# A latent attention stage with its values in runs of two units, banks split 3+3+2, and query rows laid out by transfers

## What is computed

```python
Wdkv = x @ latent_w + latent_b
q = jnp.einsum('btc,hcl->bhtl', x, Wd_w) + Wd_b[None, :, None, :]
scores = jnp.einsum('bhtl,bsl->bhts', q, Wdkv) / jnp.asarray(np.sqrt(d_head), dtype=x.dtype)
scores = jnp.where(causal[None, None, :, :], scores, -jnp.inf)
attn = jax.nn.softmax(scores, axis=-1)
y = jnp.einsum('bhts,bsl->bhtl', attn, Wdkv)
z = jnp.transpose(y, (0, 2, 1, 3)).reshape(b, t, h * Wdkv.shape[-1])
return z @ out_w + out_b
```

## Time and profile before

| | |
|---|---|
| median of three executions | 3189.93 us (3189.91 to 3198.72) |
| the profiled execution: time | 3197.16 us |
| its span, first to last instruction | 3195.4 us |
| latent attention in it, from its first transposes to its last output | about 2105 to 3080 us |
| mean granted TensorE clock | 0.919 of full speed |

### The profile page before, as it was taken

The page is one execution under the profiler, slowest core; times in us unless marked ns, Lnnn a source line. Parts: engine busy times, 40 slices in busy tenths (PEclk is TensorE's granted clock), DMA queues, the critical chain, the costliest instruction groups (busy, mean ns, idle before and its releaser), DMA issues. The chain is left out here.

```text
span 3195.4 us, 55424 instructions
## 1 busy us (share of the span) xinstructions
PE 2832.2 (89%) x15400; PEld 1924.1 (60%) x15400; DVE 2087.3 (65%) x5242; ACT 1199.9 (38%) x2164; POOL 836.7 (26%) x1220
## 2 busy tenths in 40 slices
PE   5999999958787888689999998869989989999986
PEld 4777777735555555467777776445465465465453
DVE  6777777747676777577777776355556556555533
ACT  2111111127565657521111111335545545545532
POOL 1222332225555555423222332001101101111100
PEclk8999999958888788899999998879999999999988
DMA  3000000000000000110000000000000000000000
GB/s 130 0 0 0 0 0 0 1 0 2 3 2 3 2 2 2 61 44 0 0 0 0 0 0 1 0 1 1 1 2 1 1 1 1 1 1 1 1 1 27
DMA packets 12996, 23.60 MB, mean 7 GB/s; under 512 B 2306, under 2 KB 7682, under 8 KB 12804
## 3 DMA queue, kind: packets, MB, share of 16 engines
q1 hardware_dynamic: 12804, 21.22, 2.0%
HBM read 18.52 MB, written 2.10 MB: 6 GB/s over the span
## 5 line engine op out<-in xcount | busy, mean ns | idle before, releaser
L555 DVE SCALAR_TENSOR_TENSOR moe_acc<-moe_ps,moe_comb,moe_acc 128x512 f32<-128x512 f32 x896 | 661.1, 744 | 174.5 <-PE moe_ps L304 167.9
L2017 DVE CUSTOM_DVE_ANT_0 attn_masked<-attn_psm,attn_causal 128x1024 f32<-128x1024 f32 (+7 forms) x512 | 367.6, 755 | 210.4 <-PE attn_psm L1742 199.3
L1921 ACT ACTIVATE attn_probs<-attn_pse 128x512 f32<-128x512 f32 (+1 forms) x640 | 319.9, 553 | 301.6 <-PE attn_pse L1756 301.0
L304 PE MATMUL moe_ps<-moe_Wg,moe_xh 128*128 128x512 f32 x1024 | 329.4, 403 | 25.0 <-DVE moe_Wu L501 25.0
L335 PE MATMUL moe_ps<-moe_Wd,moe_ih 128*128 128x512 f32 x1024 | 337.8, 411 | 0.0
L304 PE MATMUL moe_ps<-moe_Wu,moe_xh 128*128 128x512 f32 x1024 | 337.1, 411 | 0.0
L1772 PE MATMUL attn_psy<-attn_probs,attn_V 128*64 128x512 f32 (+3 forms) x1536 | 325.5, 524 | 0.3 <-POOL attn_probs L1677 0.3
L454 POOL TENSOR_SCALAR moe_part<-consts,moe_pick,moe_prob 128x8 f32<-128x8 f32 x256 | 98.1, 398 | 752.1 <-ACT moe_prob L389 752.1
L1677 POOL TENSOR_SCALAR_AFFINE_SELECT attn_probs<-attn_probs 128x256 f32<-128x256 f32 (+1 forms) x192 | 95.1, 495 | 757.7 <-ACT attn_probs L1921 757.7
L1021 POOL TENSOR_TENSOR attn_R<-attn_R 128x1024 f32<-128x1024 f32 (+1 forms) x128 | 215.5, 1690 | 201.6 <-DVE attn_R L1365 201.4
L1756 PE MATMUL attn_pse<-attn_qS,attn_kS 110*128 110x512 f32 (+3 forms) x768 | 233.2, 394 | 21.4 <-ACT attn_probs L1921 15.2
(11 more groups left out here) (208 smaller groups left out, 4871.2 us busy)
## 6 DMA issues: line engine op xcount, KB each, us to landing
moe_stageg<-in_w_gate SPq DMA_DIRECT2D x8, 512.0 KB, 7.2
moe_stageu<-in_w_up SPq DMA_DIRECT2D x8, 512.0 KB, 8.3
moe_stageg<-in_w_down SPq DMA_DIRECT2D x8, 512.0 KB, 3.7
out<-X SPq DMA_DIRECT2D x1, 2048.0 KB, 8.9
attn_qS<-attn_mh SPq DMA_DIRECT2D x64, 4.0 KB
attn_qS<-attn_ml SPq DMA_DIRECT2D x64, 4.0 KB
attn_wd<-in_wd SPq DMA_DIRECT2D x1, 864.0 KB, 5.7
attn_w<-in_wqkv SPq DMA_DIRECT2D x1, 768.0 KB, 5.1
```

Source lines behind the costliest of these rows:

```text
L304: last = pe.matmul(expert_bank[j % 4][:, :], a[q][:, :], w[b][:, cols], start=k == 0, stop=k == 2)
L555: dve.scalar_tensor_tensor(acc[:, q, r, :], expert_bank[j % 4][:, :], comb[:, q, r, e:e + 1], acc[:, q, r, :], ALU.mult, ALU.add).then_inc ...
L1921: act.activation(probs[:, u % 2, c, HALF - n:HALF], e_bank[c][:, HALF - n:HALF], ACT.Exp, scale=SCORE_SCALE).then_inc(p_ready, 1)
L2017: dve.tensor_tensor_reduce(masked[:, k % 2, 0:n], m_all[:, base:base + n], causal[:, SEQ - n:SEQ], 1.0, NEG, ALU.add, ALU.max, mx[:, q, v: ...
```

## The change

It rewrites the latent attention only.

- **PSUM.** The eight banks were 4 for maxima and projection, 2 for scores, 1 for sums, 1 for the rest. They are now 3 (`m_all`), 3 (`e_all`, a ring over the scores) and 2 (`y_all`, one for each half). `probs` is a ring of four units. The turned maxima and the output projection use part of the third bank of `m_all`; a wide tile of the maxima uses its first two, a small one the third.
- **Order on TensorE.** A pair is five steps of two units. A step makes three scores, two tiles of maxima, the fourth score, and then the values of two units in one run. The last two units' values are made in the next pair, behind its first scores. The half with seven units comes first (`HALVES`).
- **Queries.** One projection a pair, three pairs ahead: 6 matmuls of 512 columns with 72 stationary columns (both heads, not repeated), straight from `wd`. ScalarE writes the high part (`qH`) and VectorE the low one (`qL`), two calls each. SP then fills the 108 rows of each head by transfers, six for each half of the queries (`queries`), 36 rows of 512 numbers each: those of the first half once pair m no longer reads it, those of the second half after pair m's last score. Between the two halves stand the four transfers of the maxima. The tiles n = 0 and n = 1 of the maxima wait for the transfers of the first and of the second half (`q_in`).
- **Loops.** The eight pairs of an element are written out; the loop over elements stays.
- GpSimd's copies of weights are gone; `wd` is a third as wide. The opening of the next element is spread over the pairs 5 and 6 (`OPENS`), its keys and the first projection at the start of pair 6.

The core of the diff:

```diff
+        m_all = ctx.enter_context(nc.psum_tensor(f"{tag}_psm", [P, 3 * HALF], F32))
+        e_all = ctx.enter_context(nc.psum_tensor(f"{tag}_pse", [P, 3 * HALF], F32))
+        y_all = ctx.enter_context(nc.psum_tensor(f"{tag}_psy", [P, 2 * HALF], F32))
+        m_bank = [m_all[:, i * HALF:(i + 1) * HALF] for i in range(3)]
+        y_bank = [y_all[:, i * HALF:(i + 1) * HALF] for i in range(2)]
...
+        HALVES = (1, 0)
+        units = [(s, u) for s in HALVES for u in tile_units(s)]
+        NU, NE = len(units), 2 * len(units)
+        N1 = len(tile_units(1))
         DIAGONAL = [u for u in range(NU) if units[u][1][0][4]]
         PRODUCTS = ((0, 0), (1, 0), (0, 1))
+        STEPS = NU // 2
+        QUERY_TILE = [8 * c + j for c in range(2) for wide, small in ((7, 1), (6, 2), (5, 3), (4, 0)) for j in (wide, small)]
...
+        def e_part(k, lo, hi):
+
+            return e_all[:, (k % 3) * HALF + lo:(k % 3) * HALF + hi]
+
+        def ring(q, u):
+
+            return (u + 2 * q) % RING
+
+        def o_part(j, rows, n):
+
+            return m_all[0:rows, 2 * HALF + (j % 2) * P:2 * HALF + (j % 2) * P + n]
...
-                with eng.Fori(0, PAIRS // 2 - 1) as i:
-                    for q in range(2):
-                        pair(b * PAIRS + i * 2 + q, q, i * 2 + q, b, (True, True))
-                pair(b * PAIRS + PAIRS - 2, 0, PAIRS - 2, b, (True, more))
-                pair(b * PAIRS + PAIRS - 1, 1, PAIRS - 1, b, (more, more))
+                for i in range(PAIRS):
+                    pair(b * PAIRS + i, i, b, more)
...
-                def pair(m, q, i, b, ahead):
-                    if ahead[0]:
+                def queries(p, q, h):
+
+                    s = HALVES[h]
+                    half = slice(s * HALF, (s + 1) * HALF)
+                    sp.wait_ge(qs_ready, after(p * 2 + h))
+                    for c in range(2):
+                        rows = slice(c * LAT, (c + 1) * LAT)
+                        for part, src in enumerate((qH, qH, qL)):
+                            sp.dma_start(f32(qS[q][c][part * LAT:(part + 1) * LAT, half]), f32(src[q][rows, half])).then_inc(q_in[q][h], 16)
+
+                def start():
+                    for p in range(2):
+                        for h in range(2):
+                            queries(p, p, h)
+                    maxima(0, 0)
+
+                def pair(m, i, b, more):
+                    q = i % 2
+                    if follows(i, 2, more):
+                        sp.wait_ge(s_ready, after(m * NE + 2 * N1 - 1))
+                        sp.sem_inc(sp_pause, 1)
+                        queries(m + 2, q, 0)
+                    if follows(i, 1, more):
                         maxima(m + 1, 1 - q)
-
-                pipeline(sp, lambda: maxima(0, 0), pair, lambda b, more: None)
+                    if follows(i, 2, more):
+                        sp.wait_ge(s_ready, after(m * NE + NE - 1))
+                        sp.sem_inc(sp_pause, 1)
+                        queries(m + 2, q, 1)
...
-                def project(m, c):
-                    pe.wait_ge(wq_ready, after(m))
-                    pe.wait_ge(mx_ready, after((m - 1) * 16 + 15))
-                    for s in range(2):
+
+                def project(p, i):
+                    for h, s in enumerate(HALVES):
+                        pe.wait_ge(qs_ready, after((p - 1) * 2 + h))
                         for k, (a, w) in enumerate(PRODUCTS):
-                            last = pe.matmul(m_bank[2 * c + s][0:STACK, :], wcur[:, w, c * STACK:(c + 1) * STACK],
+                            last = pe.matmul(m_bank[h][0:2 * LAT, :], wd[w][:, i * 2 * LAT:(i + 1) * 2 * LAT],
...
-                        pe.wait_ge(qs_ready, after(m * 4 + 1 + 2 * n))
-                    else:
-                        pe.wait_ge(mx_ready, after(m * 16 + n - 2))
+                        pe.wait_ge(q_in[q][n], (m - q) * 48 + 96)
+                    pe.wait_ge(mx_ready, after(m * 16 + n - 2))
...
+                def scores(m, q, u, c):
                     s, pieces = units[u]
-                    for c in range(2):
-                        pe.wait_ge(p_ready, after(m * 2 * NU + 2 * (u - 1) + c))
-                        for k, (kt, at_, qc, n, _) in enumerate(pieces):
-                            last = pe.matmul(e_bank[c][:, at_:at_ + n], kS[:, kt * P:(kt + 1) * P],
-                                             qS[q][c][:, s * HALF + qc:s * HALF + qc + n], start=True, stop=True)
-                        last.then_inc(s_ready, 1)
+                    k = 2 * u + c
+                    if u == 0 and c == 0:
+                        pe.wait_ge(m_in, (m + 1) * 64)
+                    pe.wait_ge(p_ready, after(m * NE + k - 3 if k >= 3 else (m - 1) * NE + (18, 19, 17)[k]))
+                    for kt, at_, qc, n, _ in pieces:
+                        last = pe.matmul(e_part(k, at_, at_ + n), kS[:, kt * P:(kt + 1) * P],
+                                         qS[q][c][:, s * HALF + qc:s * HALF + qc + n], start=True, stop=True)
+                    last.then_inc(s_ready, 1)
...
+                    opening = more and i == OPENS + 1
+                    keys = kN if i == PAIRS - 1 else kS
+
+                    def maximum(k):
+                        if not ahead:
+                            return
+                        if k == 0:
+                            if follows(i, 2, more):
+                                pe.wait_ge(qs_ready, after((m + 2) * 2 + 1))
+                            pe.wait_ge(ml_ready, after(m))
+                            if opening:
+                                pe.wait_ge(v_ready, after(b + 1))
+                        for n in (2 * k, 2 * k + 1):
+                            scores_max(m + 1, 1 - q, n, keys)
+
+                    for d in range(STEPS):
+                        if d == 0 and opening:
+                            latents(b + 1)
+                        if d >= 1:
+                            maximum(2 * d - 1)
+                        for u, c in ((2 * d, 0), (2 * d, 1), (2 * d + 1, 0)):
+                            scores(m, q, u, c)
+                        if d == 0 and opening:
+                            pe.wait_ge(ml_ready, after(m))
+                            latent_rows(b + 1)
+                        if d < STEPS - 1 and not (d == 0 and opening):
+                            maximum(2 * d)
+                        scores(m, q, 2 * d + 1, 1)
+                        if d == STEPS - 1:
+                            if ahead:
                                 transpose_max(m + 1, 1 - q)
+                            if more and i == OPENS:
                                 transpose_x(b + 1)
+                            if projected(i, more):
+                                project(m + 3, (i + 3) % PAIRS)
+                        if d == 0:
+                            if i > 0:
+                                for u in (NU - 2, NU - 1):
+                                    values(m - 1, 1 - q, u)
+                            if opening:
+                                pe.wait_ge(ks_ready, after(b * 2 + 3))
+                                project(m + 2, 0)
+                                maximum(0)
+                        else:
+                            for u in (2 * d - 2, 2 * d - 1):
+                                values(m, q, u)
+                    if i == PAIRS - 1:
+                        for u in (NU - 2, NU - 1):
+                            values(m, q, u)
...
+                def high_query(p, i, staged):
+                    for h, s in enumerate(HALVES):
+                        act.wait_ge(qp_ready, after(p * 2 + h))
+                        if staged:
+                            act.wait_ge(q_in[i % 2][h], (p - i % 2) * 48)
+                        act.activation(qH[i % 2][:, s * HALF:(s + 1) * HALF], m_bank[h][0:2 * LAT, :], ACT.Identity,
+                                       bias=q_bias[:, i:i + 1]).then_inc(qt_ready, 1)
...
+                def low_query(p, i):
+                    for h, s in enumerate(HALVES):
+                        half = slice(s * HALF, (s + 1) * HALF)
+                        dve.wait_ge(qt_ready, after(p * 2 + h))
+                        dve.scalar_tensor_tensor(qL[i % 2][:, half], m_bank[h][0:2 * LAT, :], q_bias[:, i:i + 1],
+                                                 f32(qH[i % 2][:, half]), ALU.add, ALU.subtract).then_inc(qs_ready, 1)
...
+RING = 4
+OPENS = PAIRS - 3
```

More of the change, by code:

```diff
@@ L1546, in attn1_phase @@
         VN = sb("VN", [P, BT, LAT])
-        wcur = sb("wcur", [P, 2, 2 * STACK], F32R)
-        bcur = sb("bcur", [STACK, 2, 2])
-        qT = sb("qT", [STACK, 2, HALF], F32R)
+        qH = [sb(f"qH{q}", [2 * LAT, SEQ], F32R) for q in range(2)]
+        qL = [sb(f"qL{q}", [2 * LAT, SEQ], F32R) for q in range(2)]
         qS = [[sb(f"qS{q}{c}", [KROWS, SEQ], F32R) for c in range(2)] for q in range(2)]
@@ L1605, in pipeline, with follows, projected @@
             element(BATCH - 1, False)
```

(62 more changed lines are left out.)

258 lines of the change are left out of this document (111 added, 147 removed).

## The result

The changed kernel takes 3348.24 us (median of four, 3342.87 to 3356.68), the kernel before 3189.92 beside it: ratio 1.0499, 95% interval 1.0461 to 1.0537. It is 158 us slower, where 122 were forecast, inside the range of 3235 to 3370.

A forecast was written before the change was run, and what follows sets the result against it. TensorE, with its waits, was taken as the bound. A boundary pair of 29.3 us (21.5 work, 2.2, 1.9 and 2.7 waits, 1.0 clock) gave, with start, openings and end, +122 on 3190: 3312, range 3235 to 3370.

The forecast's parts named there:

- TensorE's own work: Latent attention, per pair: 23.75 less 1.63 for halved projections and 0.6 for merged runs of values, giving 21.5 us.
- waits inside the pair: TensorE waits for the maxima: 0.7, 0.3 and 0.6 in steps 1 to 3, 0.6 in step 4; together 2.2 us.
- first wait, maxima's transfers: Pair boundary: maxima land 5.52 us after the turning starts, 3.6 of cover is left, so TensorE waits 1.9.
- second wait, query rows: Before tile n = 1: ten SP transfers at 0.67 us each land at 9.5, TensorE stands at 6.8 and waits 2.7.
- Both bounds: Issue time of a 36-row transfer: 0.43 + 0.04 below, 0.95 us above, putting the second wait between 0.9 and 4.4.
- clock: Behind the two boundary waits the granted clock falls, adding 1.0 us a pair; one such fall had cost 1.2.
- A clock dearer than 1.0: Stated sign of being wrong: a clock that falls twice a pair costs more than the 1.0 us added.
- An opening pair: Opening of the next element: adds 8.1 us of work, fills 4.6 of waits once, gives back 3 for a serial chain.
- 1: Rival: boundary transfers are hidden, so the kernel is faster, 3105 to 3165 us; chance 0.10.
- 3: Rival: query rows land with the maxima, only the wait for the maxima bites, 25.6 a pair, 3215 to 3250; chance 0.10.
- 2: Rival: no change, the landing at about 6.0 us, 1.3 of saved work against as much waiting; chance 0.03.
- 4: Rival: SP's queue is the bound, 36-row transfers take 0.95 us or more, a pair 31.5, 3370 and above; chance 0.08.

The follow-up runs named there:

- `sets4`: Changed kernel with four sets of stacked queries instead of two, all query transfers issued at a pair's start: 3197.26 us, ratio 1.0026 to the kernel before.
- `double`: Changed kernel with each of the six second-half query transfers cut into two of 256 columns, same bytes: 3443.73 us, ratio 1.0789 to the kernel before.
- `filler`: Changed kernel with idle matmuls ahead of TensorE's two boundary waits (9 and 22) in pairs 1 to 5 of each element: 3310.0 us, ratio 1.0385.
- `best1`: Changed kernel with four query sets, the first two maxima tiles ahead of a pair's first score, and values one unit at a time: 3185.95 us, ratio 0.9981.
- `unrolled`: Kernel before with only the six pairs that stood in a loop written out: 3169.98 us, ratio 0.9937 to the kernel before.

## Why the prediction was right, step by step

The forecast of a pair at a boundary was 29.3; measured are 30.47. Three terms came out 1.5 lower together than forecast and two 2.5 higher, so that part of the closeness of the sum is luck. Term by term (forecast, then measured in the pair 2264.49 to 2294.96 and its neighbour):

| term | forecast | measured |
|---|---|---|
| TensorE's own work | 21.5 | 21.14 (`sets4`) |
| waits inside the pair | 2.2 | 1.6 (1.3 for maxima, 0.3 for an exponential) |
| first wait, maxima's transfers | 1.9 | 1.4 |
| second wait, query rows | 2.7 | 3.75 |
| clock | 1.0 | 2.5 (23.68 less 21.14) |

- **Own work.** Six projections take 1.56 from start to start (2294.04 to 2295.60), as forecast. A merged run saves 0.14, forecast 0.15.
- **Waits inside the pair.** 0.59, 0.25 and 0.50 for maxima in this pair and 0.50, 0.60 and 0.50 in its neighbour, and in both 0.31 ahead of the turning, whose releaser is ScalarE and not, as forecast, VectorE: 1.6 and 1.9. At full clock (`sets4`) those for maxima are 0.74, 0.61 and 0.51; the slow stretch swallows part of the first one.
- **First wait.** Landing 1.88 as in the earlier trace rows; SP's first transfer is issued 0.95 behind the turning, where I had carried over 1.61. That is why the wait is 1.4 and not 1.9. In the earlier trace rows the issue stood later by 0.66, and the traces show where: ScalarE's first step on the maxima (`mh`) starts 1.02 behind the turning there (2455.48), behind two exponentials that its program has ahead of it, and 0.36 behind the turning here (2294.37), ahead of the last exponential.
- **Second wait: undersized by 1.05.** Taken at 0.67, a transfer of 36 rows of 2 KB costs 0.75 to 0.79 of the queue, and the last one is used 2.38 behind its issue, not 1.89. From the first maxima transfer the chain is 9.2 long (2294.96 to 2304.14), where the forecast had 9 x 0.67 + 1.89 = 7.9: 0.5 of the difference is the landing, 0.5 the five intervals between the six transfers of the queries (3.85 for 3.35), 0.3 the four before them (2.95 for 2.68). Both bounds held: 3.75 lies in the range of 0.9 to 4.4. `sets4` shows the mechanism, `double` the slope.
- **Clock: undersized by half or more, and the term that was mis-sized most.** A clock dearer than 1.0 was among the signs of being wrong, and it came. I took the cost of one wait of 1.59 (1.2) and rounded down for two. Two waits of 1.36 and 3.75 with 1.5 of work between them brought 3.66 us at 0.50 and 3.2 more at 0.76. In busy time it is 2.5; net of the shorter wait for the maxima behind it, 2.0; `filler` gives 2.1.
- **The sum.** From one pair's first maxima transfer to that of seven pairs on, 183.3 became 219.3 in the first element (2173.83 on), +36.0 where 28.9 were forecast; the third element +36.0, the second +39.7 with its `finish`, the last +35.1 (forecast 30.4). Together 146.8, forecast 117: the 30 between them are nearly the 1.2 of each of 27 pairs. An opening pair takes 36.4, forecast 29.3 + 8.1 - 4.6 + 3 = 35.8. Start, first pair and the other two `finish` give +1.5, forecast +5, and the end -0.6. That is the 147.6 of the profiled executions. The median moved by 158, because the profiled execution of before stands 7 over its median and that of after 3 under.
- **Rivals.** 1 and 3 fell: the transfers are not hidden, nor issued in 0.43. 2 fell with them: the plain pairs took 30 us and not 24.8. 4 did not come either: a transfer takes 0.77, nearer to 0.67 than to the 0.95 from which it counted. That rival was priced too high, though: with six transfers at 0.95 the forecast's own sum gives a pair of 31.0, not 31.5, and some 3360, inside the range of the forecast.
- **The Trainium skill.** The sentence cited from DMA: Bandwidth & Descriptors (Issuing engines are not separate DMA queues), by which the issuing time is usually small beside the transfer, helps little in this queue: an issue of 0.77 is a third of the 2.38 from issue to use, and ten in a row take 7.5 us, against 2.4 for the last landing; in `double` each further issue took 0.76 with no further byte. The rule of the same page on many small transfers (Rules for kernel authors), to make one large one of them, agrees with that row; here it holds for transfers of 72 KB already, above the 64 KB under which the page sees mostly overhead.

What stays open: why the landing of 36 rows of 2 KB takes 0.5 more than that of the maxima (halving the rows' length in `double` took 0.3 of it, but rows and bytes were not varied apart), and why `sets4` loses the clock behind its one wait in three pairs of 24, and `best1` at some boundaries and not at others, where the rows read alike.

## What to carry to other kernels

Count the transfers that stand behind a release at the end of a stage, multiply by the queue's time for one, and compare with the work that is left to cover them; two further sets of buffers that let them be issued earlier were worth 151 us of the 158 lost against the kernel before (of the 178 against `unrolled`), without one byte less. Price a wait on TensorE with what the clock takes behind it (here 2 us a pair, behind 5 of waiting), and look for a second wait close behind the first: here the plain pairs with both lost clock every time (0.83 to 0.94 over the pair), those with one of 1.4 in three cases of 24. A run that groups like work saves little (0.14) when the group in between was what another engine needed as time.

## What the runs showed of the hardware

- An SBUF to SBUF transfer of 36 rows of 2 KB costs 0.75 to 0.79 us of SP's queue, and 0.76 with rows of 1 KB (`double`); one of 4 KB (the maxima) costs 0.67 to 0.70.
- A wait of 1.38 alone, once a pair, left the granted clock at 1.00 for the whole pair in 21 pairs of 24, and brought it down in the other three (0.93 to 0.94 over the pair, 1.6 us lost; `sets4`). Waits of 0.89 and 0.59 with 0.84 of work between them brought it down behind some boundaries (0.93 over the pair, 1.6 us lost; `best1`), and 0.81 and 0.66 behind others did not. Waits of 1.35 and 8.02 (`double`) cost no more clock than 1.36 and 3.75.
- Idle matmuls that fill the first wait and all but 1.22 of the second kept the full clock, and made the kernel 38 us faster (`filler`).
